# The first pair of a cross-attention and expert kernel: another order of loads, preparation and first products

## The reference

```python
def xattn(query, key, value, ...):
    q = rope(heads(query @ q_w.T + q_b)) * 16 ** -0.5
    k = rope(heads(key @ k_w.T + k_b))
    v = heads(value @ v_w.T + v_b)
    # query s sees keys s-64 .. s
    probs = softmax(where(seen, q @ k.T, -inf))
    return (probs @ v) @ o_w.T + o_b

def ffn(x, router_w, gate_w, up_w, down_w):
    topk_p, topk_i = top_k(softmax(x @ router_w.T), 2)      # normalised over the two
    for e in range(8):
        mask = (topk_i == e).any(-1)
        mean_w = sum of expert e's weights / count of its tokens
        out += mask * (silu(x @ gate_w[e].T) * (x @ up_w[e].T)) @ down_w[e].T * mean_w

x = x + xattn(layernorm(x), ctx, ctx, ...)
x = x + ffn(layernorm(x), ...)
```

## Time and profile before

| | us |
|---|---|
| median of 3 runs | 486.79 |
| lowest and highest of them | 485.64, 487.36 |
| the profiled execution, its own time | 483.92 |
| its span (first to last instruction) | 482.1 |
| PE busy | 446.3 (93% of the span) |
| DVE busy | 301.0 (62%) |
| ACT busy | 272.6 (57%) |
| POOL busy | 142.0 (29%) |
| granted clock of PE, mean | 0.982 |

### The profile page before, as it was taken

One profiled execution on the slowest core, in us unless ns is written; L12 is line 12 of the kernel. 1 busy time (PEld: TensorE's weight loads), 2 busy tenths in 40 slices (PEclk: granted clock), 3 DMA queues, 4 the chain that ended last, 5 costly groups with the idle time before them and its releaser, 6 DMA issues.

```text
span 482.1 us, 8983 instructions
## 1 busy us (share of the span) xinstructions
PE 446.3 (93%) x2787; PEld 367.9 (76%) x2787; DVE 301.0 (62%) x735; ACT 272.6 (57%) x863; POOL 142.0 (29%) x174
## 2 busy tenths in 40 slices
PE   3898999999999999889999999999999999999980
PEld 2655666757565655569899999999999999999980
DVE  2565769898979878775737647466465473763330
ACT  1286887878788888335445545455464554554230
POOL 5111013544446262673023050140410502205013
PEclk9999999999999999989999999999999999999995
DMA  8173421111202020229956545565465553213002
GB/s 229 41 210 111 175 78 33 39 41 33 67 6 67 8 63 26 84 76 384 300 151 155 180 78 170 166 125 164 111 164 154 89 170 94 27 40 41 0 5 34
DMA packets 24588, 50.48 MB, mean 105 GB/s; under 512 B 5410, under 2 KB 15302, under 8 KB 24394
## 3 DMA queue, kind: packets, MB, share of 16 engines
q10 hardware_dynamic: 7886, 26.44, 17.6%
q1 hardware_dynamic: 10508, 16.47, 11.3%
q0 software_dynamic: 6144, 6.97, 8.8%
HBM read 39.62 MB, written 13.20 MB: 110 GB/s over the span
## 4 chain that ended last, share of the span: by engine, by line
PE 69%; DVE 7%; ACT 7%; DMA 5%; issue 5%; POOL 3%; ACTq 1%; POOLq 0%; SPq 0%; DVEq 0%
PE b_o L703 9%; PE b_small L703 8%; PE b_s L690 7%; PE b_s L692 7%; PE b_s L691 7%; PE b_s L445 6%; ACT probs L831 4%; PE b_pv L468 3%; PE b_proj L523 3%; PE b_pt L454 3%; PE b_pt L690 2%; PE b_pt L692 2%; PE b_pt L691 2%; PE b_proj L499 2%; DMA xin<-slots 2%
## 5 line engine op out<-in xcount | busy, mean ns | idle before, releaser
L831 ACT ACTIVATE probs<-b_s,negmax 100x100 f32<-100x100 f32 x256 | 85.4, 359 | 24.1 <-DVE negmax L1108 16.7
L1320 POOL DMA_INDIRECT out<-y_sb,idnow x32 | 49.7, 1552 | 158.7 <-ACT y_sb L869 151.4
L857 ACT CAST h_hi<-h_sb 128x448 fp32r<-128x448 f32 x64 | 36.3, 567 | 88.1 <-DVE h_sb L1185 88.1
L690 PE MATMUL b_s<-x_hi,w_hi 128*128 128x448 f32 x192 | 71.5, 372 | 0.0
L692 PE MATMUL b_s<-x_hi,w_lo 128*128 128x448 f32 x192 | 70.4, 367 | 0.0
L691 PE MATMUL b_s<-x_lo,w_hi 128*128 128x448 f32 x192 | 70.0, 364 | 0.0
L1086 DVE TENSOR_TENSOR w_lo<-w_raw,w_hi 128x1024 fp32r<-128x1024 f32 x48 | 58.8, 1225 | 13.8 <-ACT w_hi L792 13.4
L1189 DVE TENSOR_TENSOR h_lo<-h_sb,h_hi 128x448 fp32r<-128x448 f32 x64 | 40.0, 625 | 40.5 <-ACT h_hi L857 39.9
L831 ACT ACTIVATION_READ_ACCUMULATOR probs<-b_s,negmax 100x1 f32 x256 | 56.5, 221 | 0.0
L445 PE MATMUL b_s<-kblk,qrot 128*100 128x400 f32 x128 | 53.7, 500 | 0.0
L792 ACT CAST w_hi<-w_raw 128x1024 fp32r<-128x1024 f32 x48 | 50.4, 1050 | 0.0
(11 more groups left out here) (153 smaller groups left out, 969.5 us busy)
## 6 DMA issues: line engine op xcount, KB each, us to landing
w_raw<-in_ffw ACTq DMA_DIRECT2D x48, 512.0 KB, 3.9
xin<-slots SPq DMA_DIRECT2D x10, 449.8 KB, 4.4
slots<-in_padrows SPq DMA_DIRECT2D x9, 449.8 KB, 4.1
kblk<-krot SPq DMA_DIRECT2D x128, 12.5 KB
out<-x_all SPq DMA_DIRECT2D x8, 200.0 KB
ctx_all<-in_ctxT SPq DMA_DIRECT2D x1, 1200.0 KB, 6.5
x_all<-in_x SPq DMA_DIRECT2D x1, 1200.0 KB
attw<-in_wT ACTq DMA_DIRECT2D x2, 256.0 KB, 3.9
```

The lines of the kernel that those rows point to most:

```text
L690: pe.matmul(o, wh[:, c, cols], x_hi[:, c, :], start=(c == 0), stop=False)
L831: m = nc.scalar.activation(probs[:, N % 3, h, :], b_s[N % 3][0:S, h * S:(h + 1) * S], ACT.Exp, bias=negmax[:, N % 4, h:h + 1], accum_out=p ...
L857: nc.scalar.copy(h_hi[:, f, :], h_sb[:, f % 2, :]).then_inc(s_hhi, 1)
L1320: G.indirect_dma_start(out, bass.IndirectOffsetOnAxis(idnow[:, n:n + 1], 0), y_sb[:, n, :], None, bounds_check=TOK + TILE - 1, oob_is_err= ...
```

## The change

It reorders what is done before the first scores.

- A tile `blank` of zeros (DVE clears it first). PE multiplies it with itself into a PSUM bank that the scores overwrite later: 16 such empty products of 128x400 ahead of `k_project`, 8 before the transposes, 2 before `q_project`, 3 behind it.
- ACT runs one exponential of one element right behind its first three DMA issues, which loads the function table there.
- DVE no longer waits for `cst` and casts before `xn_write`; `ident_bf` and `mask_bf` are written by ACT behind the first projection's evacuation, `tri_bf` and `ones_bf` by DVE behind the query's rotation.
- The eight key blocks of c = 0 of pair 0 are written by DVE (a multiplication of all 128 partitions with a column that is one in the head's partitions, new in `cst`), four behind the key rotation and four behind the query rotation. SP copies only the eight of c = 1.
- `wq` has a semaphore of its own (`s_wq`). The loads of `wv` and `wo`, `biasrow`, `rw_sb` and `rows_sb` move from ACT to SP, which issues them after `cst` has landed, ahead of pair 1's loads. `q_project` waits for `s_wq` alone, `v_project`, `v_write` and POOL's addition of a bias wait for the four.

The core of the diff:

```diff
@@ sync
             sp.dma_start(cst[:, :], consts).then_inc(s_cst, 16)
+            sp.wait_ge(s_cst, 16)
+            sp.dma_start(attw[:, 2:4], wT[:, 2:4]).then_inc(s_w, 16)
+            sp.dma_start(biasrow[:, :, :], brow).then_inc(s_w, 16)
+            sp.dma_start(rw_sb[:, :, :], rwT).then_inc(s_w, 16)
+            sp.dma_start(rows_sb[:, :], rownum).then_inc(s_w, 16)
             load_rows(1, 1, 2)
...
-                for c in range(DC):
+                for c in range(0 if i else 1, DC):
                     for h in range(HC):
@@ tensor
+                if N == 0:
+                    pe.wait_ge(s_setup, 2)
+                    pe.wait_ge(s_kblk[c], 16 * QH)
+                elif n in (0, HC // QH) or N == 1:
                     pe.wait_ge(s_kblk[c], 16 * HC * (i + 1))
...
             def q_project(i):
                 if i == 0:
-                    pe.wait_ge(s_w, 16 * 5)
+                    pe.wait_ge(s_wq, 16)
...
             def v_project(i):
+                if i == 0:
+                    pe.wait_ge(s_w, 16 * 4)
...
+            def idle(count):
+                for _ in range(count):
+                    pe.matmul(b_s[0][:, 0:QH * S], blank[:, 0:P], blank[:, :], start=True, stop=True)
+
+            pe.wait_ge(s_blank, 1)
+            idle(16)
@@ scalar
-            a.dma_start(attw[:, 0], wT[:, 0]).then_inc(s_w, 16)
-            a.dma_start(biasrow[:, :, :], brow).then_inc(s_w, 16)
-            a.dma_start(attw[:, 2:4], wT[:, 2:4]).then_inc(s_w, 16)
-            a.dma_start(rw_sb[:, :, :], rwT).then_inc(s_w, 16)
-            a.dma_start(rows_sb[:, :], rownum).then_inc(s_w, 16)
+            a.dma_start(attw[:, 0], wT[:, 0]).then_inc(s_wq, 16)
+            a.wait_ge(s_blank, 1)
+            nc.scalar.activation(table[:, :], blank[0:1, 0:1], ACT.Exp)
...
+                    if n == 0 and i < 0:
+                        a.wait_ge(s_cst, 16)
+                        nc.scalar.copy(ident_bf[:, :], cst[:, C_ID:C_ID + P]).then_inc(s_setup, 1)
+                        nc.scalar.copy(mask_bf[:, :, :], cst[:, C_MASK:C_MASK + S].unsqueeze(1)
+                                       .to_broadcast([P, QH, S])).then_inc(s_setup, 1)
@@ vector
+            V.memset(blank[:, :], 0.0).then_inc(s_blank, 1)
...
+            def first_key_blocks(half):
+                v.wait_ge(s_krot, 1)
+                v.wait_ge(s_zero, 3)
+                for h in range(half * QH, (half + 1) * QH):
+                    V.tensor_scalar(kblk[:, 0, 0, h, :], krot[:, 0:2, :].rearrange("p b s -> p (b s)"),
+                                    cst[:, C_HEAD + h:C_HEAD + h + 1], None, ALU.mult).then_inc(s_kblk[0], 16)
...
             xn_stats(0)
+            xn_write(0)
             v.wait_ge(s_cst, 16)
-            V.tensor_copy(ident_bf[:, :], cst[:, C_ID:C_ID + P]).then_inc(s_setup, 1)
-            V.tensor_copy(tri_bf[:, :], cst[:, C_TRI:C_TRI + P]).then_inc(s_setup, 1)
-            V.tensor_copy(ones_bf[:, :], cst[:, C_ONE:C_ONE + P]).then_inc(s_setup, 1)
-            V.tensor_copy(mask_bf[:, :, :],
-                          bc(cst[:, C_MASK:C_MASK + S].unsqueeze(1), [P, QH, S])).then_inc(s_setup, 1)
+            k_rotate(0)
+            first_key_blocks(0)
+            q_rotate(0)
+            first_key_blocks(1)
+            V.tensor_copy(tri_bf[:, :], cst[:, C_TRI:C_TRI + P]).then_inc(s_setup2, 1)
+            V.tensor_copy(ones_bf[:, :], cst[:, C_ONE:C_ONE + P]).then_inc(s_setup2, 1)
```

More of the change, by code:

```diff
@@ L61 @@
 C_LT = C_THR + E * MAXT
-C_ALL = C_LT + (E + 1) * E
+C_HEAD = C_LT + (E + 1) * E
+C_ALL = C_HEAD + HC
 def shape_constants():
@@ L249, in build @@
         s_wk = sem("s_wk")
+        s_wq = sem("s_wq")
+        s_blank = sem("s_blank")
         s_w = sem("s_w")
@@ L254, in build @@
         s_setup = sem("s_setup")
+        s_setup2 = sem("s_setup2")
         s_zero = sem("s_zero")
@@ L567, in ranks @@
             def ranks(i):
+                if i == 0:
+                    pe.wait_ge(s_setup2, 2)
                 pe.wait_ge(s_ch, i + 1)
@@ L634, in _ @@
                     if n == 3 and nxt:
+                        if i < 0:
+                            idle(2)
                         q_project(i + 1)
+                        if i < 0:
+                            idle(3)
                     if 0 <= N - 2 < NQ * NPAIR:
@@ L646, in _ @@
                     if n == 1 and nxt:
+                        if i < 0:
+                            idle(8)
                         xn_transpose(i + 1)
@@ L1110, in _ @@
                                         AX.X, ALU.max, negate=True).then_inc(s_max, 1)
-                    if n == 0 and nxt:
+                    if n == 0 and nxt and i >= 0:
                         xn_write(i + 1)
@@ L1125, in _ @@
                         attend(2 * i - 1)
-                    if n == (0 if i < 0 else 2) and nxt:
+                    if n == 2 and nxt and i >= 0:
                         k_rotate(i + 1)
@@ L1142, in _ @@
                         destinations(i - 2)
-                    if n == 5 and nxt:
+                    if n == 5 and nxt and i >= 0:
                         q_rotate(i + 1)
@@ L1164, in _ @@
             link(V.tensor_tensor(upto[:, :, :], bc(ntile[:, :].unsqueeze(1), [1, E + 1, E]),
-                                 cst[0:1, C_LT:C_ALL].rearrange("p (j e) -> p j e", e=E), ALU.mult))
+                                 cst[0:1, C_LT:C_HEAD].rearrange("p (j e) -> p j e", e=E), ALU.mult))
             link(V.tensor_reduce(first_f[:, :], upto[:, :, :], AX.X, ALU.add))
```

10 lines of the change are left out of this document (5 added, 5 removed).

## The result

Four runs of the changed kernel have a median of 481.65 us (479.70 to 482.91), beside 487.08 us for the kernel before (485.64 to 489.95): a ratio of 0.989, 95% interval 0.9854 to 0.9926, 5.4 us less. The forecast was 483.2, 3.6 us less, with a range from 481.7 to 485.3; the result lies at its very low edge.

The account below looks back on a forecast made before the run. PE was taken as full from about 28 us and half empty before, so the first pair's path to `v_sb` counts: 1.22, 0.34, 0.25, 1.51 and 0.32 give 3.6 us, 486.8 to 483.2 us, range 481.7 to 485.3.

Parts of the forecast that it names:

- The sign: Whole kernel: faster by more than about 1.5 us at 0.86, slower by more at 0.05, within at 0.09.
- Rows first, 1.22: First pair's normalised rows: `xn` starts when `rstd` is done, 9.22 instead of 10.44, 1.22 us less.
- The clock terms, 0.34 and 1.51: First pair at PE's upper clock level: transposes 0.90 to 0.56, queries' projection 3.03 to 1.52 us.
- rival (3): PE's clock does not rise on empty products, which only stand in the way: 487.5 to 490.2 us; chance 0.03.
- The queries' wait, 0.25: Queries' projection waits for `wq` alone, starting 0.04 behind the copy instead of 0.29: 0.25 us less.
- From rotation to `v_sb`, 3.54: Query rotation's start to `v_sb`, DVE now latest: rotation 2.25, four key blocks 1.02, two casts 0.27; 0.32 us less.
- The key blocks: Second four on DVE ahead of `v_sb`: 0.255 us each, 1.02 together; first four just covered before the query rotation.
- The late weights: SP's loads behind `cst`: `cst` lands at 7.9, last weight at 14.6; values may start until 15.2, so no cost.
- Rivals (1) and (2): Late weights delay values: (1) landing towards 18.4, 484.5 to 486.4 us, chance 0.08; (2) `cst` at 9.75, 488.2, chance 0.03.
- The third scores: First pair: key DMAs run from 12.5 to 17.5, third scores need them at 21.1, so no wait for DMA.
- Behind the first pair: Later pairs: nothing changes and PE is full, so the 3.6 us shift of `v_sb` stays whole.
- Rival (4): Part of the shift is lost later, in a wait taken to move along: 1.5 us left, 485.3 us; chance 0.06.

Follow-up runs that it names:

- before_again: The kernel before, unchanged, run once more for a second profile: that one execution took 486.24 us, span 484.4 us.
- casts_first: The changed kernel, but DVE again waits for the constants and does all four casts ahead of the normalised rows: 481.04 us, ratio 0.9884.
- no_empty: The changed kernel without its 29 empty products, the tile still cleared: 482.63 us, ratio 0.9913 to the kernel before.
- loads_act: The changed kernel, but ACT issues the four late weight loads again and SP does not wait for the constants: 479.85 us, ratio 0.9864.
- only_empty: The kernel before with only the cleared tile and the 29 empty products added: 486.07 us, ratio 1.0005.
- load_late: The changed kernel, but SP issues the 2.4 MB load of pairs 2 to 7 only after the third maximum: 486.85 us, ratio 0.9986.

## Why the prediction was right, and where it was not

**The sign** was right, as the chances had it (0.86 for faster), and the size lies in the range. That it does is partly luck. The sum was made of the wrong two halves: it gave the first pair 3.6 us and the rest nothing. The first pair gave 2.4, and the other 3.0 came behind it, at a place that the prediction had set at zero.

**Rows first, 1.22.** `xn` came 0.62 earlier, not 1.22, for the rows themselves landed 0.6 later in that execution (7.53, and 6.93 before; before_again has 7.56 with the old kernel, so this is the spread of the landing). Counted from the landing it is 3.51 to 2.29, the 1.22 of the sum. But casts_first shows that it isn't the casts' removal alone: the constants, with four loads fewer beside them, land 0.9 earlier, and with that the casts could have stayed where they were.

**The clock terms, 0.34 and 1.51,** measured 0.37 and 1.44. Their cause was put down to the empty products, and rival (3) was made to hang on it. no_empty reaches the upper level for the same instructions without them, and before_again has transposes in 0.53 and values in 1.97 with queries in 2.99: the level in the first 20 us differs from one execution to the next in the kernel before as well.

**The queries' wait, 0.25,** gave 0.19: the two empty products lie under the copy, but PE starts the queries 0.1 behind the copy's end, not 0.04.

**From rotation to `v_sb`, 3.54,** took 4.05 (14.29 to 18.34). This term was mis-sized: POOL's addition was counted among what is hidden, since "its first reader is the residual of pair 0, far behind", and it stood in DVE's way for 0.64. The key blocks were priced well: four in 1.02, 0.25 apart. The rule of the Trainium skill on two fp32 results per cycle, page "VectorE: DVE Perf Modes", section "Mode 2×_2P", doesn't hold for this tensor_scalar: by it, as the prediction worked out, four would have taken about 0.6, an estimate.

**The late weights** landed near 14.4; 14.6 was taken. The constants landed at 8.8 and not 7.9, and four issues on SP took 0.33 to 0.43 instead of 0.65; the two errors cancelled. The values' projection waited 0.42 for them, at no cost of its own; but this landing put POOL's addition beside the queries' rotation, which in loads_act, with 13.3, it hardly touched. Rivals (1) and (2) did not come about. The third scores wait for no DMA, as forecast.

**Behind the first pair** is the step that failed: "loads of pairs 2 to 7 are issued at 17.5 instead of 23.6, earlier by more than their use". The issue time was nearly right (17.94). But the load's own use was the wrong question: what matters is who is queued behind it. The key blocks of pair 1 were, and the first scores of pair 1 waited for them. So `v_sb` was no mark by which the rest moves. It moved by 3.2 in only_empty and by 2.7 in load_late, and both have the time of before: their first scores of pair 1 start at 40.05 and 39.24, near before's 39.65. Rival (4), a part of the shift lost later, had the mechanism the wrong way round: before had a later wait, and the change took it away together with the start. From the shift of `v_sb` alone one has 2.4; with the wait at pair 1 it is 3.0 in the first profile of before and 3.7 against before_again (40.38 to 36.68). Up to 5.4 there remain 1.7 to 2.4. The profiled execution of after had both clock falls, of which the first cost about 1.6, and was the slowest of its four. The mean granted clock is on record for every execution: 0.971 in this one and 0.981 to 0.982 in the other three, so these spent less time at the lower level. But between the kernels it hardly differs: the median is 0.981 for the ten executions of the changed kernel, and 0.978 to 0.979 for before on each of the three chips. A difference of 0.002 to 0.0025 is 1.9 to 2.4 us more at half clock; by the price of the fall above (1.6 us for 3.4 us at half clock) that is worth about 1 us, an estimate. Where the other 1 us or so of the gain comes from stays open.

## What to carry to other kernels

Before a stage is made faster, look for the next place whose start is tied to something else, a bulk load above all: ask what is issued behind it on the same queue and who counts on that. Here moving the load back by 5.7 us cost 5.5 us, a fall of the clock included, as much as the whole change had gained; an earlier place in the queue than the changed kernel's was not tried. Where a pause of 2 us is in a stream of products, its cost had two values here, with or without a fall of the clock, so compare medians of several runs, and use profiles for the marks between two pauses only.

## What the runs showed of the hardware

- Key-block DMAs of 12.5 KB behind a load of 2.4 MB on the same queue: those of pair 1 took 5.1 to 5.9 us in the median from issue to landing where the load had been issued 3.4 to 5.2 us ahead of the first of them, and 2.3 to 3.2 where it had been 8.5 to 9.7. Over all pairs the median is 1.8.
- A multiplication on DVE with two SBUF operands stood still while POOL added two SBUF operands, and ended 0.42 to 0.44 us behind POOL in six executions: 1.07 to 1.49 us instead of 0.57. Where POOL came second, it took 1.41 to 1.53 instead of 1.27, in three.
- PE's clock fell from 2.4 to 1.2 GHz (granted 1.00 to 0.50) behind a pause of 1.84 to 1.94 us in six profiles and not in five others with 1.77 to 1.92; it also fell behind the one of 2.63 in after_again. A fall cost 1.5 to 1.8 us there, and 2.8 behind the pause of 2.81 in load_late.
- The rows of pair 0 landed 1.8 us earlier as the first transfer on SP's queue than as the second (5.48 against 7.32), and the constants behind it 0.9 earlier, with the same bytes in all; one execution of each.
